# Attention over eight sequences: where the next sequence's projections, the maxima and one copy stand in the order of work

## The reference

```
x = x + attention0(x, mask)              # 16 heads of 16 rows, over the 512 columns, softmax, keys masked
x = x + attention1(x, cond)              # rms norm, scale and shift, qkv, heads of 32, q and k normalised, W_out
x = x + gru(cond, x)                     # 256 recurrent steps, state (8, 512)
x = x + block_attention(x)               # 8 block sums, attention over them, layer norm
```

## Time and profile before

| | us |
|---|---|
| median of 3 runs | 2042.67 (2038.59 to 2048.41) |
| the profiled execution | 2046.4 |
| its span, first to last instruction | 2044.5 |
| attention, to the first work of the recurrence | about 1106 |
| recurrence | about 890 |
| PE busy | 1888.7 (92%) |
| DVE busy | 1254.8 (61%) |
| ACT busy | 1096.4 (54%) |

### The profile page before, as it was taken

How to read it: one execution, slowest core, us unless ns; L and a number is a source line. 1 busy time by engine, 2 the same in 40 slices (tenths; PEclk the granted TensorE clock), 3 DMA queues, 4 the chain that set the end, 5 groups by cost and what they waited for, 6 DMA issues and landing times. The chain is left out here.

```text
span 2044.5 us, 87065 instructions
## 1 busy us (share of the span) xinstructions
PE 1888.7 (92%) x33006; PEld 1403.1 (69%) x33006; DVE 1254.8 (61%) x5543; ACT 1096.4 (54%) x4105; POOL 380.3 (19%) x1398
## 2 busy tenths in 40 slices
PE   8877998999989999899887999999999999999996
PEld 4234455464544635446465899999999999999995
DVE  5545383653836538364333677777777777777767
ACT  0342736637366363664744465666666666666554
POOL 3000000000000000000000234343333334343335
PEclk7788999999999999999999899999999999999997
DMA  5122213213032230412223000000000000000002
GB/s 187 68 79 52 81 30 88 74 43 95 26 95 67 52 89 22 103 44 64 82 62 106 5 0 0 0 0 0 0 0 0 0 0 0 0 0 1 0 0 83
DMA packets 103525, 86.73 MB, mean 42 GB/s; under 512 B 15616, under 2 KB 90496, under 8 KB 103440
## 3 DMA queue, kind: packets, MB, share of 16 engines
q1 hardware_dynamic: 101392, 84.38, 14.5%
q10 hardware_dynamic: 1664, 1.18, 0.2%
q0 software_dynamic: 384, 0.01, 0.0%
HBM read 60.20 MB, written 21.00 MB: 40 GB/s over the span
## 5 line engine op out<-in xcount | busy, mean ns | idle before, releaser
L1257 PE MATMUL bank_pair_A<-moving,rep 128*128 128x16 f16 x8192 | 318.0, 169 | 2.6 <-ACT bank_pair_C L1348 1.4
L1257 PE MATMUL bank_pair_C<-moving,rep 128*128 128x16 f16 x8192 | 315.7, 169 | 0.0
L1257 PE MATMUL bank_pair_B<-moving,rep 128*128 128x16 f16 x8192 | 315.6, 169 | 0.0
L1257 PEld LDWEIGHTS bank_pair_A<-moving,rep 128*128 128x128 f16 x8192 | 276.1, 96 | 13.6 <-issue 4.1
L1357 ACT ACTIVATE r_gate<-r_pre 128x16 f32<-128x16 f32 x512 | 110.5, 216 | 289.0 <-DVE r_pre L1448 289.0
L1257 PEld LDWEIGHTS bank_pair_B<-moving,rep 128*128 128x128 f16 x8192 | 259.1, 96 | 0.0
L1257 PEld LDWEIGHTS bank_pair_C<-moving,rep 128*128 128x128 f16 x8192 | 259.1, 96 | 0.0
L1244 PE MATMUL bank_pair_D<-x_part,w_in 128*128 128x256 f16 x1536 | 198.9, 275 | 7.0 <-ACT gi_rz L1384 4.4
L1139 POOL TENSOR_TENSOR x<-x,w_in 128x512 f32<-128x512 f32 x8 | 10.2, 1274 | 965.2 <-DMA w_in<-w_in 965.2
L1448 DVE TENSOR_REDUCE r_pre<-bank_pair_A 128x16 f32<-128x32 f32 x512 | 98.0, 191 | 136.9 <-PE bank_pair_A L1257 136.9
L1045 DVE TENSOR_REDUCE head_max<-bank_pair_A 128x2 f32<-128x1024 f32 x128 | 155.7, 1216 | 38.2 <-PE bank_pair_A L579 38.0
(11 more groups left out here) (262 smaller groups left out, 3767.8 us busy)
## 6 DMA issues: line engine op xcount, KB each, us to landing
rep<-parts SPq DMA_DIRECT2D x256, 64.0 KB
parts<-parts SPq DMA_DIRECT2D x48, 256.0 KB, 2.1
q_rep<-parts SPq DMA_DIRECT2D x32, 256.0 KB, 4.9
k_rep<-parts SPq DMA_DIRECT2D x64, 128.0 KB, 2.8
w_in<-in_x_dram SPq DMA_DIRECT2D x8, 512.0 KB, 4.1
x<-in_x_dram SPq DMA_DIRECT2D x8, 512.0 KB, 4.2
parts<-parts SPq DMA_DIRECT2D x32, 128.0 KB, 2.6
out_dram<-res SPq DMA_DIRECT2D x16, 256.0 KB, 2.1
```

What stands on the lines that cost most here:

```text
L1257: last = nc.tensor.matmul(ps[part][:, o:o + 2 * B], w[:, k, (first + c) * P:(first + c) * P + P], moving[j % 2][:, k, :, :].rearrange("p s ...
```

## The change

It touches the attention's lists and nothing that is computed:

- the keys' projection and its splits stand two units later (units 9 to 12, and 12, 14, 16), and so do the maxima of attention1 and their row (units 15 to 22, and 24);
- the values' projection "v0" leaves units 27 to 30 and stands at the head of the second list, after "y"; "v_aug" follows it, behind the third "score1" (in the first sequence at once);
- "y_move" is gone from ACT; SP moves the last group of y too, ahead of the load of the last group of heads;
- between the "res" steps stands one "max" instead of two, so that six of them are left for the chunks; the row of maxima is made two chunks after the last "max" (for the first sequence after the ninth "qk");
- attention1's values are projected in halves: the second block of tokens, into the second bank of pair D, stands ahead of the ninth "qk"; the first block behind it.

```diff
                 for n in range(NC * NC):
-                    at(7 + n, ("k", n))
-                at(10, ("k_full", 0))
-                at(12, ("k_hi", 0))
-                at(14, ("k_lo", 0))
-                for n in range(DC):
-                    at(27 + n, ("v0", n))
+                    at(9 + n, ("k", n))
+                at(12, ("k_full", 0))
+                at(14, ("k_hi", 0))
+                at(16, ("k_lo", 0))
             if b >= 1:
                 for h in range(H):
-                    at(13 + h // 2, ("max1", h))
-                at(22, ("neg1", 0), ("row1", 0))
+                    at(15 + h // 2, ("max1", h))
+                at(24, ("neg1", 0), ("row1", 0))
...
             yield "inv", G - 1
             yield "y", G - 1
+            if with_max:
+                yield from (("v0", n) for n in range(DC))
             for h in range(H):
                 yield "score1", h
-                if h == 0:
+                if h == 2 and with_max:
                     yield "v_aug", 0
-                    yield "y_move", 0
...
                 yield "res", oc
                 if oc < DC - 1:
-                    yield from maxes(2)
+                    yield from maxes(1)
...
         def rest_order(free, per_chunk):
-            done = False
+
+            last = None
             for m in range(M8):
                 yield "qk", m
+                if m - 2 == last:
+                    yield "row", 0
                 some = [("max", u) for u in islice(free, per_chunk)]
                 yield from some
                 if some and some[-1][1] == U0 - 1:
                     yield "neg", 0
-                    done = True
-                elif done:
-                    yield "row", 0
-                    done = False
+                    last = m
+            yield from (("v", n) for n in range(DC))
             yield "qk", M8
-            if done:
+            if last is not None and last >= M8 - 2:
                 yield "row", 0
             if per_chunk == 0:
                 yield "w_ih_hi", 0
-            yield from (("v", n) for n in range(DC * NC))
+            yield from (("v", n) for n in range(DC, DC * NC))
...
                     if more and g == 0:
                         load_rep(b + 1, g)
+                move_y(b, G - 1)
                 if more:
                     load_rep(b + 1, G - 1)
...
             def v_tokens(e, n):
-                tc, c = n // DC, n % DC
+                tc, c = NC - 1 - n // DC, n % DC
                 if n == 0:
+                    pe.wait_ge(qn_ok, e * M8 + (M8 - 2))
+                elif n == DC:
                     pe.wait_ge(hln_ok, e * M8 + M8)
-                if c == 0 and tc == 1:
-                    pe.wait_ge(qn_ok, e * M8 + M8)
```

More of the change, by code:

```diff
@@ L843, in inverse @@
                 nc.scalar.activation(sums[:, :], sums[:, :], ACT.Exp, scale=-1.0).then_inc(inv_ok, 1)
-            def move_last_y(b):
-                g = G - 1
-                act.wait_ge(y_ok, b * G + G)
-                for j in range(4):
-                    r = (4 * g + j) * DH0
-                    act.dma_start(y[r % P:r % P + DH0, r // P, :], y_pad[g % 2][32 * j:32 * j + DH0, :]).then_inc(ld_y[g % 2], 16)
             def token_rms(e):
@@ L922, in steps @@
                     elif kind == "v_aug":
-                        if b + 1 < B:
-                            v_part(b + 1)
-                    elif kind == "y_move":
-                        move_last_y(b)
+                        v_part(b + 1)
                     elif kind == "w_ih_hi":
```

## The result

| | before | after |
|---|---|---|
| median of four runs, us | 2040.74 (2038.59 to 2048.41) | 1994.53 (1990.01 to 1996.04) |
| the profiled execution, us | 2046.4 | 1990.01 |
| ratio after / before | | 0.9763, interval 0.9732 to 0.9795 |

The change makes the kernel faster by 46.2 us, 2.4%. The median before was 2042.67 over the three runs that the forecast started from and is 2040.74 over four. Run again beside the last experiments the changed kernel had 1991.65 (0.9757).

The account below looks back on a forecast made before the run. PE, busy 92%, sets the pace. 3.85 us per regular sequence (23 in six), 5 for the clock, 2 and 2.5 for first and last sequence, 1.5 for small waits: 34 us off 2046.4, less 3.7 to the median, 2008.7; range 1997 to 2028.

Parts of the forecast that it names:

- What bounds the kernel: Sequences 1 to 6: PE sets the pace; to win are its 10.5 us or so of waits and the lower clock's loss.
- rival A: Stalls only move: ACT paces the first list, DVE the head of the second; 2026 us, chance 0.13.
- price of v0: End of first list: of the 3.5 us of PE work that v0 takes away, only 2.1 come back, ACT becoming the bound.
- Keys: First list: PE's 1.66 us wait for the queries' low part goes, 0.85 returns; gain 1.0 us per sequence, bounds 0 and 1.7.
- v0 and y: First list gives back 2.1 us, second list's head costs 0.9; gain 1.2 us per sequence, bounds -2.3 and +2.7.
- Maxima, row, halves: "res" steps and chunks' end: waits of 0.41, 0.64 and 0.66 us go; gains 1.0 and 0.65 us per sequence.
- Clock: Six sequences: 10 us lost to the lower clock behind long waits; half taken, 5 us, bounds 0 and 10.
- First and last sequence: First gains 2 us (0 to 4); last gains 2.5 (1 to 4), its waits of 7.31 and 2.77 us going.
- The sum: Whole kernel: 3.85 us per regular sequence, 23 in six; with the other terms 34 us, giving 2008.7.
- small waits: Waits under 0.2 us that go with the removed stalls: 1.5 us over the whole kernel.
- Rival B: Row of maxima comes late, its transfer delayed beside SP's loads, next sequence's first unit waits; 16 us, 2025, chance 0.07.
- C: Slower: v0 pays its full 3.5 us in the second list, nothing comes back in the first; 2067 us, chance 0.04.

Follow-up runs that it names:

- v0 back: Changed kernel with the next values' projection and their copy back at their old places (units 27 to 30), y still on SP: 1999.3 us, ratio 0.9792.
- keys back: Changed kernel with the keys' projection and attention1's maxima two units earlier again, as before: 2005.46 us, ratio 0.9822.
- y alone: Kernel before with only the last rows of y moved by SP's queue instead of ACT: 2030.12 us, ratio 0.9932.
- v0 alone: Kernel before with only the next values projected at the head of the second list, y still on ACT: 2029.25 us, ratio 0.9923.
- the tail alone: Kernel before with only the maxima spread, their row two chunks later and attention1's values in halves: 2022.15 us, ratio 0.989.

## Why the prediction was right and wrong

**What bounds the kernel: right.** PE sets the pace; rival A, that the stalls only move, is out. 5.18 us of PE's holes went in a period. The new waits in a regular sequence are the two that were named at units 8 and 9, those at the end of the first list (0.55 and 0.46 us and a smaller one, inside the price of v0), one of 0.42 us in the head, and one of 0.29 us at unit 17.

**Keys, forecast 1.0, measured 1.9 alone and 1.67 within the change.** This is the step that failed. The term asked "what is late next" and counted what the move adds, the two waits of "some 0.4 and 0.45 us" (they came as 0.30 and 0.47), but not what it takes away further on. The keys' splits move with the projection, and their place beside ACT's inverse was put at nothing without a word; of the maxima it says that they "keep their distance to the keys' splits and to their row; I put them at nothing". What changed was the distance from the split to the inverse, which did not move: the old wait at unit 15, printed as 0.68, a hole of 0.85, went. The upper bound of 1.7 was too low as well, since it counted one of the two waits behind the moved step. The claim to have read "every wait of PE over 0.4 us" did not hold: besides this one it left out 0.56 and 0.52 in the head, 0.85 behind "tokens", 0.77 for the copy, and 0.41 at the maxima of attention1.

**v0 and y, forecast 1.2, measured 1.1.** The first list gave back 2.1 (run with v0 back; forecast 2.1), the head cost 0.98 (forecast 0.9). Right in its size and in most of its working, with some luck: it was worked out on sequence 4, whose head is 0.2 us longer, and without the two waits for DVE. What the prediction did not see is that the two halves of this term are substitutes, so that v0's move is worth next to nothing beside y on SP.

**Maxima, row, halves, forecast 1.0 + 0.65, measured 2.16.** The mechanism was right, the size was not: the three waits printed as 0.41, 0.64 and 0.66 are holes of 0.57, 0.81 and 0.83, in sum 2.2. The term took printed idle time for time.

**Clock, forecast 5, measured 10.0.** "I take half of it": the rows gave 10, and all of it came back. The half stood for doubt, not for a row. That the rows gave 10 is in part luck: two of six sequences were read, with clocks rounded to 0.01, which is 1.3 us each. The reason given, that these stretches "stand behind the two long waits that go", holds only one way: without the waits there was no half clock in any kernel, but with the keys' wait back the clock stayed full, and so it did in the heads when only the keys were moved.

**First and last sequence, forecast 2 and 2.5, measured up to 8.0 and 4.1.** Of the first part's 8.0 us 2.4 are the start, 3.7 are its first list (49.23 to 45.52), and 3.2 the stretch from the chunks to the copy, against 1.3 more in the head; the last of these varies by kernel between 55.5 and 61.2 us, so between 2.4 and 5.6 are the change's. In the last sequence the forecast named both waits; timeline, after, beside the earlier trace rows, with the first unit of sequence 1 above them:

```profile
197.39 0.61 PE L599 MATMUL bank_pair_A<-rep 128*128 128x256 f16 x4 [0.87 <-DMA rep<-max_row]
...
958.85 0.28 PE L707 MATMUL bank_pair_A<-q_rep,k_rep 128*128 128x256 f16 x1 [0.82 <-ACT probs L894]
...
963.99 0.69 DVE L991 TENSOR_TENSOR x<-x,w_in 128x512 f32<-128x512 f32 x1 [4.96 <-DMA w_in<-w_in]
```

PE's 2.77 became 0.82. y's wait did not go, it fell from 7.31 to 4.96 us.

**The sum.** For the six sequences 23 + 1.5 + 5 = 29.5 us were forecast and 41.1 measured. The difference of 11.6, to 0.1, is 0.9 x 6 = 5.4 for the keys (the first list shrank by 4.0 us; with v0's share taken as the 2.1 that were forecast, the keys' is 1.9), 0.5 x 6 = 3.1 for the printed idle times, 5.0 for the clock, less 0.5 for v0 and y and less the 1.5 of small waits, which the measured parts already hold. That is about what the medians are short by (46.2 against 34). A regular sequence, forecast at 121 to 123 us, took 119.53. The result lies 2.5 us below the range, so either the keys or the clock, had it alone been counted in full, would have moved the forecast and its range by 5 us and brought the result inside. The range was also too narrow at this end: it took the terms "at their bounds by turns", while four of them came out at or above their upper bounds together (keys 1.9 against 1.7, tail 2.16 against 1.8, clock 10.0 against 10, last sequence 4.1 against 4).

**Rival B** had its condition met: the row's transfer took 5.0 us in the median (3.9 to 6.2 for the regular sequences), where it had taken 2.1:

```profile
rep<-max_row ACTq DMA_DIRECT2D x8, 16.0 KB, 5.0
```

It stayed below the margin of 6.7 us that the prediction had worked out, though not by much, so regular sequences lose nothing; only the row that the first sequence makes, behind its ninth step, is waited for, 0.87 us. Issued behind the ninth step in every sequence, it took 2.2 to 3.4. That transfers of two issuing engines run on the same 16 DMA engines and interleave is what the Trainium skill says (DMA: Bandwidth & Descriptors, "Issuing engines are not separate DMA queues"); the 2.1 us with no load beside it and the 5.0 us beside four loads of 256 KB agree with it. **C** is out: the first list gave back 2.1 us, and PE's longest wait for DVE in the head is 0.18 us.

**What stays open** is what decides whether a wait of 1.65 us is followed by half clock. It was kept with other periods (keys back, y alone, v0 alone, the tail alone) and gave none or three in six, with the same 12.0 us ahead of it each time. A run that only shifts the attention as a whole in time was not tried. Nor were the maxima of attention1 moved by themselves, nor the later row and the copy in halves tried together.

## What to carry to other kernels

When a step is moved in a hand-written order, look up every wait behind its old place, not only the one aimed at: what its helpers did on other engines goes with it. Cost a hole by the distance between instruction starts and not by the printed idle time, and before two fillings are added up ask whether they fill the same hole. It takes both kinds of run to see it: here the parts put in alone sum to 6.1 us per period, v0, y and the keys taken out one by one to 2.05 us with 2.16 for the tail beside them, and the whole, 5.18, lies between. Time lost at half clock is a term of its own: all that the rows show can come back if every long wait goes, so count all of it and let the doubt stand in the range, and compare kernels by their stretches at full clock, since it came and went here with edits that left a wait as it was. When terms are added up, let the range hold the case that several of them are at their bounds together.

## What the hardware showed that was not expected

- A wait of 1.65 us on PE was followed by some 0.6 of the clock in three of six sequences of one kernel and in none of another, at a price of 1.6 us each (1.2 in the head), with the 12.0 us of work ahead of it the same. Where only the keys' wait was removed, the heads kept their waits of 1.40 and 1.60 us and were at full clock too.
- A transfer of 16 KB on ACT's queue went from 2.1 to 5.0 us, at most 6.2, beside four loads of 256 KB on SP's.
- The printed idle time of PE is some 0.16 us short of the hole between two matmuls, and 0.07 short behind a "pv".
